# Two items' queries in one matmul, rounds without a loop, and heads weighed four at a time in the first cross-attention of a two-layer decoder

## What is computed

```python
q = (x @ Wq).reshape(B, Nq, h, dh)
k = (context @ Wk).reshape(B, Nk, h, dh)
v = (context @ Wv).reshape(B, Nk, h, dh)
scores = jnp.einsum('bqhd,bkhd->bhqk', q, k) * scale
attn = jax.nn.softmax(scores, axis=-1)
out = jnp.einsum('bhqk,bkhd->bqhd', attn, v).reshape(B, Nq, h * dh)
return out @ Wo + bo
...
x = _layernorm(x + _L0_xattn_ref(x, ctx_768, L0_xattn_Wq, L0_xattn_Wk, L0_xattn_Wv, L0_xattn_Wo, L0_xattn_bo), axis=-1)
```

## Time and profile before

| | us |
|---|---|
| median of 3 runs | 1021.91 |
| lowest and highest | 1020.33, 1023.41 |
| the profiled execution | 1018.9 |
| its span, first to last instruction | 1017.1 |

### The profile page before, as it was taken

One profiled execution on the slowest core, in us unless ns is written; L12 is line 12 of the kernel. 1 busy time (PEld: TensorE's weight loads), 2 busy tenths in 40 slices (PEclk: granted clock), 3 DMA queues, 4 the chain that ended last, 5 costly groups with the idle time before them and its releaser, 6 DMA issues. The chain is left out here.

```text
span 1017.1 us, 17797 instructions
## 1 busy us (share of the span) xinstructions
PE 972.4 (96%) x6560; PEld 750.6 (74%) x6560; DVE 575.5 (57%) x1307; ACT 408.8 (40%) x1069; POOL 154.2 (15%) x151
## 2 busy tenths in 40 slices
PE   9899799999999999989999999989989999999985
PEld 4678677877778778768999998566667777777663
DVE  3887545555555555656755665358634444555544
ACT  3556434333343433435545454357633222332221
POOL 0423610110110100003434342300010000000000
PEclk9999899999999999998999999999999999999998
DMA  4500100000000000008511100720000000001000
GB/s 157 201 1 1 53 16 1 17 16 1 15 0 0 0 0 0 1 1 274 170 42 41 42 1 6 170 37 3 2 19 16 16 16 16 16 0 25 5 5 19
DMA packets 26814, 36.18 MB, mean 36 GB/s; under 512 B 3648, under 2 KB 22160, under 8 KB 26752
## 3 DMA queue, kind: packets, MB, share of 16 engines
q1 hardware_dynamic: 26752, 35.35, 11.6%
HBM read 30.75 MB, written 2.75 MB: 33 GB/s over the span
## 5 line engine op out<-in xcount | busy, mean ns | idle before, releaser
L1119 ACT ACTIVATE x_prob<-bank,x_negmax 112x375 f32<-112x375 f32 x128 | 72.3, 570 | 150.0 <-DVE x_negmax L1029 150.0
L1838 DVE TENSOR_TENSOR moe_h_low<-moe_sq,moe_h_high 128x512 fp32r<-128x512 f32 (+1 forms) x64 | 55.2, 884 | 52.3 <-ACT moe_h_high L1938 40.3
L1915 POOL TENSOR_TENSOR moe_sq<-moe_r 128x512 f32<-128x512 f32 (+1 forms) x64 | 63.9, 1002 | 104.7 <-ACT moe_r L1947 83.2
L1029 DVE TENSOR_REDUCE x_negmax<-bank 112x1 f32<-112x375 f32 x128 | 64.2, 543 | 9.5 <-PE bank L919 7.3
L1947 ACT ACTIVATE moe_r<-bank 128x512 f32<-128x512 f32 (+1 forms) x64 | 34.9, 546 | 74.9 <-PE bank L101 68.7
L101 PE MATMUL bank<-moe_w_low,moe_h_high 128*128 128x256 f32 x224 | 63.3, 283 | 0.0
L101 PE MATMUL bank<-moe_w_high,moe_h_low 128*128 128x256 f32 x224 | 63.3, 283 | 0.0
L101 PE MATMUL bank<-moe_w_high,moe_h_high 128*128 128x256 f32 x224 | 63.3, 283 | 0.0
L940 PEld LDWEIGHTS bank<-x_prob_t,x_v 125*64 125x64 f32 x768 | 37.2, 136 | 30.9 <-issue 26.6
L1034 DVE COPY x_prob_t<-bank 125x336 f32<-125x336 f32 x128 | 58.4, 498 | 2.0 <-PE bank L928 0.5
L919 PE MATMUL bank<-x_kt,x_qt 64*112 64x375 f32 x256 | 58.3, 521 | 1.2 <-DVE x_kt L1021 0.7
(11 more groups left out here) (370 smaller groups left out, 2267.4 us busy)
## 6 DMA issues: line engine op xcount, KB each, us to landing
moe_w<-in_L_ffn_W SPq DMA_DIRECT2D x15, 512.0 KB, 4.8
ctx_t<-in_ctx_t SPq DMA_DIRECT2D x8, 376.0 KB, 4.1
x_ctx_t<-in_ctx_t SPq DMA_DIRECT2D x8, 376.0 KB, 3.2
wk<-in_L_xattn_Wk SPq DMA_DIRECT2D x2, 1024.0 KB, 5.3
wv<-in_L_xattn_Wv SPq DMA_DIRECT2D x2, 1024.0 KB, 7.9
wq<-in_L_xattn_Wq SPq DMA_DIRECT2D x2, 1024.0 KB, 10.0
wo<-in_L_xattn_Wo SPq DMA_DIRECT2D x2, 1024.0 KB, 11.8
xt<-in_xt SPq DMA_DIRECT2D x1, 896.0 KB, 4.5
```

Of the source, the lines that this page charges most:

```text
L1029: dve.tensor_reduce(negmax[:, g:g + 1], S_BANK(u, e)[0:T, 0:S], AX_X, ALU.max, negate=True).then_inc(max_ready, 1)
L1119: act.activation(PROB(u, e)[:, :], S_BANK(u, e)[0:T, 0:S], ACT.Exp, bias=negmax[:, g:g + 1], accum_out=total[:, g:g + 1]).then_inc(p_ready, 1)
L1838: dve.tensor_tensor(h_low[half][:, m, 0:size], sq[m % 2][:, 0:size], h_high[half][:, m, 0:size].bitcast(F32), ALU.subtract).then_inc(low_d ...
L1915: pool.tensor_tensor(sq[m % 2][:, 0:size], r[m % 2][:, 0:size], r[m % 2][:, 0:size], ALU.mult).then_inc(sq_done, 1)
```

## The change

Three things change in `cross_attention`. First, the queries of items 2k and 2k + 1 are made together: a query job now covers 2 blocks of `wq` with 224 moving columns, so that four jobs of 4 matmuls make the queries of two items. Those of items 0 and 1 are all made in round -1, those of items 2k and 2k + 1 by two jobs each in unit 0 of rounds 2k - 2 and 2k - 1, and rounds 6 and 7 have none. `qt` is twice as wide and is indexed by the pair of items. Second, `rounds` writes all ten rounds out, and the jobs and their counts come from a table, `JOBS`, made ahead. Third, `WEIGHED` says which pairs are weighed in a unit: unit 1 the pair 0, unit 3 the pairs 1 and 2, unit 5 the pairs 3 and 4, unit 7 the pairs 5 and 6, and pair 7 in unit 0 as before. `prob_t` has four buffers in place of two.

```diff
+    WEIGHED = {1: (0,), 3: (1, 2), 5: (3, 4), 7: (5, 6)}
...
+        if n == 0:
+            if i < 0:
+                return [("q", (0, a)) for a in range(4)]
+            k = i // 2 + 1
+            return [("q", (k, 2 * (i % 2) + a)) for a in range(2)] if 2 * k < B else []
+        if n <= M // 2:
+            return [("k", 2 * n - 2), ("k", 2 * n - 1)]
+        return [("v", 2 * n - 2 - M), ("v", 2 * n - 1 - M)]
...
-        kt, v, qt = pair("kt", [128, M, S]), pair("v", [SP_, ST, INNER]), pair("qt", [128, M, T])
+        kt, v, qt = pair("kt", [128, M, S]), pair("v", [SP_, ST, INNER]), pair("qt", [128, M, 2 * T])
...
-        prob_t = [[sb(f"prob_t{p}{e}", [SP_, ST, T]) for e in range(PER)] for p in range(2)]
+        prob_t = [[sb(f"prob_t{p}{e}", [SP_, ST, T]) for e in range(PER)] for p in range(4)]
...
-        def rounds(eng, round_):
-            round_(-1, 1)
-            round_(0, 0)
-            with eng.Fori(0, B // 2 - 1) as j:
-                round_(2 * j + 1, 1)
-                round_(2 * j + 2, 0)
-            round_(B - 1, 1)
-            round_(B, 0)
...
+        def rounds(round_):
+            for i in range(-1, B + 1):
+                round_(i, i % 2)
...
-                        last = pe.matmul(S_BANK(u, e)[0:T, 0:S], qt[p][rows, u, :], kt[p][rows, u, :], start=True, stop=True)
+                        last = pe.matmul(S_BANK(u, e)[0:T, 0:S], qt[i // 2 % 2][rows, u, i % 2 * T:(i % 2 + 1) * T], kt[p][rows, u, :], start=True, stop=True)
...
-                        for m in range(4):
-                            last = accumulate(pe, out[:, m * T:(m + 1) * T], [
-                                (core.wq[:, c, (4 * a + m) * 128:(4 * a + m + 1) * 128], core.xt[:, c, bass.ts(i + 1, T)])
+                        k, at = a
+                        for m in range(2):
+                            last = accumulate(pe, out[:, m * 2 * T:(m + 1) * 2 * T], [
+                                (core.wq[:, c, (2 * at + m) * 128:(2 * at + m + 1) * 128], core.xt[:, c, 2 * k * T:(2 * k + 2) * T])
...
-                            if u > 0:
-                                weigh(i, u - 1, p)
+                            for w in WEIGHED.get(u, ()):
+                                weigh(i, w, p)
```

More of the change, by code:

```diff
@@ L769, in cross_attention, with parts, fronts, round_jobs @@
     RA, RB, OUT, NT = "ra", "rb", "out", "nt"
-    fronts = [("q", 0), ("q", 1)] + [("k", m) for m in range(M)] + [("v", n) for n in range(2 * ST)]
-    NF = len(fronts)
-    QK = 2 + M
     U_OUT, U_NT, U_RA = 2, 5, 6
     U_KEYS = 4
[L775 to L780, removed]
+    WEIGHED = {1: (0,), 3: (1, 2), 5: (3, 4), 7: (5, 6)}
+    assert M == U and 2 * ST == 6
+    def parts(i):
+        return 0 <= i < B, i + 1 < B, i > 0
+    def fronts(i, n):
+        if n == 0:
[6 more added lines that the diff above has]
+        return [("v", 2 * n - 2 - M), ("v", 2 * n - 1 - M)]
+    def round_jobs(i):
+        heads, front, tail = parts(i)
+        count, units = [0, 0], []
+        for n in range(U):
             now = []
@@ L786, in jobs @@
             if front:
-                now += [(f % 2, *fronts[f]) for f in (2 * n, 2 * n + 1)]
+                now += [(f % 2, *job_) for f, job_ in enumerate(fronts(i, n))]
             if tail and n == 0:
@@ L791, in jobs, with place, keys_made @@
                 now.append((0, RA, 0))
-            made = []
+            units.append([])
             for b, kind, a in now:
-                made.append((b, count[b], kind, a))
+                units[-1].append((b, count[b], kind, a))
                 count[b] += 1
-        return made
-    def place(u, what, heads, front, tail):
-        return next(n for b, n, kind, a in jobs(u, heads, front, tail) if kind == what)
+        return units
+    JOBS = {i: round_jobs(i) for i in range(-1, B + 1)}
     def before(i, b):
[L803 to L806, removed]
+        return sum(1 for r in range(-1, i) for unit in JOBS[r] for job_ in unit if job_[0] == b)
+    def place(i, what):
+        return next(n for unit in JOBS[i] for b, n, kind, a in unit if kind == what)
+    def keys_made(i, b):
+        return before(i - 1, b) + max(n for unit in JOBS[i - 1] for c, n, kind, a in unit if c == b and kind == "k") + 1
     with ExitStack() as ctx:
@@ L912, in scores @@
                     if u == 0:
-                        pe.wait_ge(job_used[0], before(i - 1, 0) + QK // 2 + (0 if isinstance(i, int) and i <= 1 else 1))
-                        pe.wait_ge(job_used[1], before(i - 1, 1) + QK // 2 + (0 if isinstance(i, int) and i <= 1 else 1))
+                        for b in range(2):
+                            pe.wait_ge(job_used[b], keys_made(i, b))
                     for e in range(PER):
@@ L989, in round_ @@
                                 scores(i + 1, 0, 1 - p)
-                            if u > 0:
-                                weigh(i, u - 1, p)
+                            for w in WEIGHED.get(u, ()):
+                                weigh(i, w, p)
                         if tail and u == 0:
                             weigh(i - 1, U - 1, 1 - p)
-                        for b, n, kind, a in jobs(u, heads, front, tail):
+                        for b, n, kind, a in JOBS[i][u]:
                             job(i, p, b, n, kind, a)
@@ L997, in round_ @@
                             scores(i + 1, 0, 1 - p)
-                rounds(pe, round_)
+                rounds(round_)
             def empty(eng, i, p, b, n, kind, a, copy):
@@ L1012, in empty @@
                 assert kind == NT
[L1013 removed]
+                return copy(core.xt[:, :, (i - 1) * T:i * T], src[:, 0:2 * T].rearrange("d (c t) -> d c t", c=KD), None)
             @block.vector
@@ L1069, in round_ @@
                     for u in range(U):
-                        if tail and u == 0 and not (isinstance(i, int) and i == B):
+                        if tail and u == 0 and i < B:
                             invert(i - 1, 1)
@@ L1088, in round_ @@
                         if tail and u == 1:
-                            divide(i - 1, 1, before(i, 0) + place(0, RB, heads, front, tail) + 1)
+                            divide(i - 1, 1, before(i, 0) + place(i, RB) + 1)
                         if heads and u == U_RA + 1:
-                            divide(i, 0, before(i, 0) + place(U_RA, RA, heads, front, tail) + 1)
-                        for b, n, kind, a in jobs(u, heads, front, tail):
+                            divide(i, 0, before(i, 0) + place(i, RA) + 1)
+                        for b, n, kind, a in JOBS[i][u]:
                             if b == 1 and kind == OUT:
@@ L1100, in round_ @@
                             row_max(i + 1, 0)
-                rounds(dve, round_)
+                rounds(round_)
             @block.scalar
@@ L1144, in _ @@
                 act.preload_act_table_set(EXP_LN)
-                rounds(act, round_)
+                rounds(round_)
 def wide_cross_attention(core, d, output):
```

13 lines of the change are left out of this document (5 added, 8 removed).

## The result

The changed kernel takes 1012.38 us (median of 6 runs, 1011.06 to 1014.02) beside 1022.41 for the kernel before on the same chip (6 runs, 1019.66 to 1024.03): a ratio of 0.9906, with the 95% interval 0.9888 to 0.9923. The forecast was 1013, between 1008 and 1018, and -8.7 us. The profiled execution took 1011.95 us with a span of 1010.1.

What follows compares the result with a forecast made beforehand. TensorE was taken to bound the stage, so work leaving it leaves the time. Terms +2.5 - 3.2 - 3.1 - 3.2 - 1.3 - 0.4 = -8.7 us from the 1021.91 us median gave 1013 us, range 1008 to 1018.

Steps and rivals of the forecast that it cites:

- The queries: Unit 0 of rounds 0 to 5: 16 wide records take 3.14 us instead of 3.67, -3.2 us in all.
- Ahead of the rounds: Queries of items 0 and 1 made before round 0, partly at half clock: 8.6 us for 6.11, +2.5 us.
- Round 6: Unit 0 has no queries to make, -3.67 us, but waiting for two heads' exps gives 0.55 back: -3.1 us.
- Merged weighs: Rounds 0 to 6: three fewer visits a round, 0.15 us saved for each of 3 x 7 merges, -3.2 us.
- Unit 5: Second value job's wait of 0.21 us for the vector engine's copy is hidden in 6 rounds, -1.3 us.
- Rounds written out: Registers, branches and register waits go; TensorE idles 0.02 us of 41.00 in the loop, so nothing to gain.
- Unit 6: Inverses wait for bank 0, which ScalarE empties at about 4.0 us, when TensorE arrives: no cost.
- Round 7: Chain of scores, maximum and exp: unit 2 loses its weigh, -0.72; later heads come together; -0.4 us in all.
- Cover gone: Rival: exps come late where weighs left; unit 4 alone 1018 us, chance 0.07; units 2, 4, 6 1028 us, 0.02.
- Code loading: Rival: written-out rounds load some seven more instruction blocks, up to 1.46 us idle each, 1023 us; chance 0.04.
- Wide columns free: Rival: weight loading alone sets the query pace, 0.115 us a record, 9.5 us more gained, 1004 us; chance 0.03.
- It doesn't do what it says: Rival: merged weighs save nothing and unit 5's wait moves with them, -4.2 us, 1018 us; chance 0.08.

Runs made afterwards that it cites:

- the halves: Against the kernel before, both with rounds written out: queries for two items but single weighs, 1016.0 us; merged weighs but one item's queries per matmul, 1012.7 us.
- The 56 and 168 columns: Query matmuls moving 56 of 112 columns in the otherwise unchanged written-out kernel, 1021.19 us; 168 of 224 in the changed kernel, 1005.95 us.
- the single edits: Against the kernel before: rounds written out only, 1019.88 us; that plus queries for two items, 1016.0 us; written out plus merged weighs, 1012.7 us.

## Why the prediction was right, point by point

**What bounds the kernel** held: apart from the waits named below every job on TensorE kept its length, so what left TensorE left the stage, and the halves added up.

**The queries** came as worked out, 3.13 against 3.14, from a row of the same shape in another stage. The 56 and 168 columns say why it was the right row to ask. Counting matmuls would have given half of the time, scaling by columns nothing: at 112 columns the pace doesn't depend on them (it is put down to the weights), at 224 it does, and the gain is the distance of two narrow records, 2 x 0.115, to a wide one, 0.189. The estimate by the Trainium skill ("TensorE: Matmul & The Clock Gate", "Back-to-back issue gap") would have had 16 records in 2.2 us, 1.2 times 1.84; they take 3.13, and the measurement decides.

**Ahead of the rounds** 8.55 against 8.6. This term is the loosest: it moves with the moment at which the clock rises. The wide queries took 8.69, 8.39, 8.85 and 7.75 us in four other executions, the narrow ones 5.19, 6.16 and 5.15 in three. The change could have come out anywhere between +1.6 and +3.7, so that it came within 0.1 is luck.

**Round 6** gave back 0.65 where 0.55 was forecast; the waits are the two that were named.

**Merged weighs** gave 0.15 for each, as forecast, and unit 4 takes 3.38, from 240.06 to 243.44, with the heads in time:

```profile
240.06 0.81 PE L935 MATMUL bank<-const,x_prob 112*125 112x112 f32 x6
...
242.78 0.19 ACT L1128 ACTIVATION_READ_ACCUMULATOR x_prob<-bank,x_negmax 112x1 f32 x1
...
243.33 0.20 ACT L1128 ACTIVATION_READ_ACCUMULATOR x_prob<-bank,x_negmax 112x1 f32 x1
...
243.44 0.81 PE L935 MATMUL bank<-const,x_prob 112*125 112x112 f32 x6
```

The forecast of no wait held, but the step under it was wrong: "the second is wanted about 0.35 later than the first, at 3.74". It is wanted at about 3.55, and the margin is 0.07 to 0.08 us where 0.27 was read.

**Where it missed.** Four places of the sum were off, two each way: -0.5 in unit 5, -0.6 in unit 2, +0.5 in unit 6 and +0.3 in round 7. That they nearly cancel is chance.

*Unit 5*, -1.8 for -1.3. The idle of 0.21 that was read in the earlier trace rows is gone, but so is what follows a wait: the first record behind it takes 0.33 us, and 0.23 without a wait. Before, in round 1, the record that follows the one behind the wait:

```profile
207.77 0.40 PE L101 MATMUL bank<-wv_low,ctx_high 128*125 128x512 f32 x1
```

That is 0.33 behind the 207.44 of the earlier trace rows. After, round 2, with nothing waited for:

```profile
246.84 0.34 DVE L1030 COPY xt<-bank 128x224 f32<-128x224 f32 x1
...
247.48 0.40 PE L101 MATMUL bank<-wv_rest_low,ctx_rest 128*125 128x512 f32 x1
247.71 0.39 PE L101 MATMUL bank<-wv_high,ctx_high 128*125 128x512 f32 x1
247.94 0.39 PE L101 MATMUL bank<-wv_low,ctx_high 128*125 128x512 f32 x1
```

The term should have been 0.44 + 0.33 - 2 x 0.23 = 0.31. By the single edits 0.10 of it is the loop's and 0.20 the merged weigh's: 2.70 before, 2.60 written out, 2.40 with the weighs merged.

*Rounds written out*, -1.3 for 0: unit 2's 0.10 and the loop's part of unit 5, in six rounds each (0.6 of it stands in the row of unit 5). The failed step is "In the loop TensorE is idle 0.02 us of 41.00, so there is nothing to gain on it". The busy column counts records to their modelled ends, which lie over the start of the next; a wait shorter than that overlap doesn't show in it. The idle of the weight loads does, 2.8 and 1.0 us over six rounds, and it was at hand.

*Unit 6*, +0.5 for nothing. ScalarE's copy out of bank 0 ends at 212.86 in round 1, and the inverses' weights wait for it:

```profile
212.28 0.58 ACT L1119 COPY x_v<-bank 125x512 f32<-125x512 f32 x1
...
212.91 0.39 PEld L973 LDWEIGHTS bank<-const,x_inv 112*128 112x128 f32 x4 [0.30 <-ACT x_v L1119]
212.91 0.60 PE L973 MATMUL bank<-const,x_inv 112*128 112x112 f32 x4
```

The prediction named this wait, put the two at the same moment and took that for no cost. The weight load starts 0.05 us behind the end of the copy, together with its matmul instead of ahead of it, and the second record follows 0.15 behind the first where it was 0.10. The inverses take 0.44 for 0.38, 0.06 of the 0.07 a round.

*Round 7*, -0.1 for -0.4. Unit 2 lost 0.90, its weigh and a little more. The merged weigh of unit 5 stands in the chain of scores and exps there and gives 0.45 back (that unit takes 3.30 us, 2.85 before), and the three head pairs at the end take 1.88 where two took 1.48. Two take 1.30 without a wait, so 0.18 of the third pair's 0.58 was hidden in the wait for the last copies, where half was expected to be, and 0.40 was not.

**The rivals.** Cover gone: false here, and nearer than its condition said: it decides from exps 0.07 to 0.08 us later, not from 0.27. Code loading: false, with the blocks there. The clock low for all of the queries ahead: false, it rose after 5.0 us. Wide columns free: false, shown at two widths. It doesn't do what it says: false.

## What to carry to other kernels

Price a widened matmul by a row of the same shape, wherever in the program it stands: here two records of 112 columns took 0.23 us and one of 224 took 0.20, neither half nor the same. Merging visits of small matmuls gains their fixed part (0.15 us here), but a visit also covers someone else's chain, so read how much cover remains, from the end of that chain to the weight load that waits for it and not to a guessed part of a turn: here 0.27 us was read and 0.07 to 0.08 was left. A deliberate delay measures it, if the lateness is taken at the end of the chain and not from the length of what was put in. Look for waits in the idle of the weight loads, since a TensorE that is busy 40.98 of 41.00 us still had 0.4 us a round to give in units 2 and 5; and compare a stage with itself, since the same code elsewhere varied by 4.6 us with the clock.

## What the runs showed of the hardware that was not expected

- An f32 matmul record with 128 weight columns takes 0.113 us at 56 and 0.114 at 112 moving columns, 0.149 at 168 and 0.196 at 224 (each with the job's fixed part in it); within a job the records start 0.112, 0.112, 0.142 and 0.189 apart.
- In this loop the vector engine comes some 0.1 us later to work that TensorE waits for: the residual add starts 0.58 us behind the key job's start in the loop and 0.46 written out, and the copy of the turned input, which opens the second value job, is 0.10 later too. As said, which part of the loop takes it is open.
- Behind a wait the next 512-column record takes 0.33 us instead of 0.23, so a wait of 0.2 us costs 0.3.
- Straight code of six rounds in place of a loop of two brought nine more instruction blocks in the stage (19 for 10), and TensorE didn't stop for one of them.
- The first weight load of a turn's second head starts 0.22 us behind the turn's first matmul, so its exp is wanted well before the 0.37 at which half of the turn is over.
